# The high/low split of P^T and y^T writes their 32-token blocks as rows of 128

## The reference

```
# layer 0
Q = x @ Wq + bq ; K = ctx @ Wk + bk ; V = ctx @ Wv + bv
weights  = softmax(Q @ K^T * 512**-0.5, axis=keys)
x1 = x + (weights @ V) @ Wo + bo
# layer 1
q = x1 @ Wq + bq ; k = ctx @ Wk + bk ; v = ctx @ Wv + bv
w    = softmax(q @ k^T / sqrt(512), axis=tokens of x1)
x2   = x1 + w @ v
out  = (x2 - mean) * rsqrt(var + 1e-6) * gamma + beta      # over features
```

## Time and profile before

| | |
|---|---|
| three runs | 1252.03, 1254.40, 1256.06 us; median 1254.4 us |
| the profiled execution | 1254.56 us; its span 1252.8 us |
| TensorE busy (matmuls) | 1212.8 us, 97% of the span, 8304 matmuls |
| GpSimd, VectorE, ScalarE busy | 927.1, 892.0, 700.2 us |
| granted TensorE clock, mean | 0.987 |
| DMA | 241.36 MB, mean 193 GB/s |

### The profile page before, as it was taken

The page is one execution under the profiler, slowest core; times in us unless marked ns, Lnnn a source line. Parts: engine busy times, 40 slices in busy tenths (PEclk is TensorE's granted clock), DMA queues, the critical chain, the costliest instruction groups (busy, mean ns, idle before and its releaser), DMA issues.

```text
span 1252.8 us, 25385 instructions
## 1 busy us (share of the span) xinstructions
PE 1212.8 (97%) x8304; PEld 1122.5 (90%) x8304; DVE 892.0 (71%) x1874; ACT 700.2 (56%) x1545; POOL 927.1 (74%) x713
## 2 busy tenths in 40 slices
PE   6989999999999999999999999999999999999984
PEld 5779999999999999999999999999999999999973
DVE  1457777777777777777777777777777777767763
ACT  2436565655656565565656566555656655565542
POOL 2436778778877877787787778778777877877664
PEclk8999999999999999999999999999999999999988
DMA  8346666656655665665666566556655655665431
GB/s 327 108 137 211 187 197 214 206 173 216 219 185 197 212 210 172 213 220 178 204 210 212 170 212 222 186 195 212 216 169 206 224 193 186 215 199 176 151 118 50
DMA packets 121727, 241.36 MB, mean 193 GB/s; under 512 B 13920, under 2 KB 79456, under 8 KB 113120
## 3 DMA queue, kind: packets, MB, share of 16 engines
q1 hardware_dynamic: 120816, 240.18, 57.6%
q10 hardware_dynamic: 880, 0.79, 0.2%
HBM read 157.03 MB, written 83.89 MB: 192 GB/s over the span
## 4 chain that ended last, share of the span: by engine, by line
PE 89%; DMA 3%; DVE 3%; POOL 2%; issue 2%; ACT 1%; SPq 1%; ACTq 0%; POOLq 0%; DVEq 0%
PE bank L268 82%; PE bank L385 2%; PE bank L358 2%; DMA beta_b<-in_beta 1%; PE bank L337 1%; DMA yT_raw<-y_dram 1%; DVE stats L795 1%; DMA y_dram<-y_blk 1%; SPq L214 1%; PE bank L395 1%; PE bank L401 1%; DVE R L787 0%; POOL Y L956 0%; POOL yT_lo L908 0%; DVE y_blk L725 0%
## 5 line engine op out<-in xcount | busy, mean ns | idle before, releaser
L908 POOL TENSOR_TENSOR PT_lo<-PT_raw,PT_hi 128x512 fp32r<-128x512 f32 x64 | 82.7, 1292 | 192.4 <-ACT PT_hi L475 192.4
L596 ACT ACTIVATE Y<-R,nmr,rstd 128x512 f32<-128x512 f32 x128 | 97.4, 809 | 184.1 <-POOL nmr L948 184.1
L908 POOL TENSOR_TENSOR xT_lo<-IN,xT_hi 128x1024 fp32r<-128x1024 f32 x64 | 154.2, 2409 | 24.3 <-ACT xT_hi L475 24.3
L908 POOL TENSOR_TENSOR yT_lo<-yT_raw,yT_hi 128x1024 fp32r<-128x1024 f32 x64 | 154.4, 2412 | 23.2 <-ACT yT_hi L475 23.2
L956 POOL TENSOR_TENSOR Y<-Y,gamma_b 128x512 f32<-128x512 f32 x128 | 162.4, 1289 | 3.7 <-ACT Y L596 3.7
L959 POOL TENSOR_TENSOR Y<-Y,beta_b 128x512 f32<-128x512 f32 x128 | 163.1, 1297 | 0.0
L268 PE MATMUL bank<-yT_hi,A_hi 128*128 128x256 f32 x512 | 146.6, 286 | 5.4 <-POOL yT_lo L908 5.4
L268 PE MATMUL bank<-yT_hi,A_lo 128*128 128x256 f32 x512 | 147.4, 288 | 0.0
L268 PE MATMUL bank<-yT_lo,A_hi 128*128 128x256 f32 x512 | 146.7, 286 | 0.0
L268 PE MATMUL bank<-xT_hi,A_hi 128*128 128x256 f32 x512 | 144.1, 281 | 0.0
L268 PE MATMUL bank<-xT_lo,A_hi 128*128 128x256 f32 x512 | 144.0, 281 | 0.0
(11 more groups left out here) (116 smaller groups left out, 4204.8 us busy)
## 6 DMA issues: line engine op xcount, KB each, us to landing
IN<-in_packed SPq DMA_DIRECT2D x64, 1024.0 KB, 5.7
R<-in_x SPq DMA_DIRECT2D x64, 512.0 KB, 6.3
y_dram<-y_blk SPq DMA_DIRECT2D x256, 128.0 KB, 2.4
yT_raw<-y_dram SPq DMA_DIRECT2D x64, 512.0 KB, 3.6
out<-Y SPq DMA_DIRECT2D x64, 512.0 KB, 3.4
E_dram<-E_blk SPq DMA_DIRECT2D x256, 64.0 KB, 1.8
PT_raw<-E_dram SPq DMA_DIRECT2D x64, 256.0 KB, 2.6
WqT_s<-in_WqT SPq DMA_DIRECT2D x2, 1024.0 KB, 11.3
```

Source lines behind the costliest of these rows:

```text
L596: nc.scalar.activation(Y[n.k % 2][:, q, :], R[n.k % 4][:, q, :], ACT.Identity, bias=nmr[:, q:q + 1], scale=rstd[:, q:q + 1]).then_inc(Y_se ...
L908: return nc.gpsimd.tensor_tensor(dst, src, fp(hi), ALU.subtract)
```

## The change

The tensors `PT_hi`, `PT_lo`, `yT_hi` and `yT_lo` get the shape depth-and-half (q, k) x 128 tokens. The copy and the subtraction read `PT_raw` and `yT_raw` in the order (q k), i, t, which is 32-element runs (16 for P^T, 32 for y^T) at a stride, and write rows of 128 contiguous tokens; the subtraction reads the high part in that same contiguous order. `by_q` gives TensorE 2 runs of 128 contiguous elements in place of 2 x 4 runs of 32. Numbers of instructions, sizes of tensors, DMAs, waits and order stay.

```
-        PT = split("PT", [P, NB * ST, LT, 32])
+        PT = split("PT", [P, ST * LT, P])
-        yT = split("yT", [P, NB * ST, DT, 32])
+        yT = split("yT", [P, ST * DT, P])
...
         def by_q(t, k):
-            return t[:, :, k, :].rearrange("p (i q) t -> p q i t", q=ST)
+            return t[:, :, :].rearrange("p (q k) t -> p q k t", q=ST)[:, :, k, :]
+
+        def raw(t):
+            return t[:, :, :, :].rearrange("p (i q) k t -> p i (q k) t", q=ST).rearrange("p i c t -> p c i t")
+
+        def blocks(t):
+            return t[:, :, :].rearrange("p c (i t) -> p c i t", i=NB)
...
-                copy(flat4(PT[0]), flat4(PT_raw)).then_inc(PT_hi, 1)
+                copy(blocks(PT[0]), raw(PT_raw)).then_inc(PT_hi, 1)
...
-                copy(flat4(yT[0]), flat4(yT_raw)).then_inc(yT_hi, 1)
+                copy(blocks(yT[0]), raw(yT_raw)).then_inc(yT_hi, 1)
...
-                minus(flat4(PT[1]), flat4(PT_raw), flat4(PT[0])).then_inc(PT_lo, 1)
+                minus(blocks(PT[1]), raw(PT_raw), blocks(PT[0])).then_inc(PT_lo, 1)
...
-                minus(flat4(yT[1]), flat4(yT_raw), flat4(yT[0])).then_inc(yT_lo, 1)
+                minus(blocks(yT[1]), raw(yT_raw), blocks(yT[0])).then_inc(yT_lo, 1)
```

## The result

The changed kernel took 1248.2 us (median of 8 runs, 1246.89 to 1250.8) against 1254.3 us before (8 runs, 1252.03 to 1256.84): ratio 0.9949, 95% interval 0.9938 to 0.9959. It is 6.1 us faster (the interval says 5.1 to 7.8); forecast were 6.2. The profiled execution took 1247.58 us, its span 1245.8 against 1252.8.

A forecast was written before the change was run, and what follows sets the result against it. TensorE's matmul starts were taken as the bound, GpSimd's loop next. `v_` and `Pc_` together -0.10 us per body over 61 bodies, given as -6.2 us, other engines' costs covered: 1254.4 to 1248.2 us, range 1244.5 to 1256.5.

The forecast's parts named there:

- What bounds the kernel: Steady part: distances between TensorE matmul starts set the time, 18.24 us per body; GpSimd's loop second at 17.75 us.
- `v_`: 24 matmuls moving y^T: longer runs bring them near the pace of `u_`, saving 0.094 us per body.
- `Pc_`: 12 matmuls moving P^T: longer runs save 0.01 us per body, from one slow 0.13 us distance in each half.
- 6/7: Share of the 0.11 us gain counted for `v_`, as 1 of 7 joins between runs stays.
- ScalarE and GpSimd at nothing: Strided reads in copies and subtractions: 0.03 us growth on each engine, all covered by slack.
- Rival 2: GpSimd subtractions pay per run, slower: 29 us at 20 ns per run, some 475 us at 172 ns; chance 0.12.
- the loop that it would have hit: GpSimd, norm, `PT_hi`, `PT_lo` waiting on each other: 17.75 us per body, 0.49 us of slack.
- the pause before `rstd`: GpSimd's slack in its loop, 0.49 us per body; expected to shrink to about 0.36 us.
- Rival 1: Layout never set the matmul pace of `v_`: no change or small gains, 1254 us expected; chance 0.33.
- Rival 3: TensorE's new moving rows meet worse addresses, slower: +19 us, 1273 us; chance 0.03.

The follow-up runs named there:

- e1: Changed kernel with only y^T in rows of 128, P^T copied and read as before: 1251.36 us, ratio 0.9972 to the kernel before.
- e2: Changed kernel with only P^T in rows of 128, y^T as before: 1252.3 us, ratio 0.9989 to the kernel before.
- e4: Changed kernel with VectorE's transposes reordering blocks so products read one run of 256: 1248.85 us, ratio 0.9958 to the kernel before.
- e5: Changed kernel with `v_` and `Pc_` reading 4 runs of 64, elements in wrong order: 1247.94 us, one run.
- e8: Changed kernel with stationary matrices A0 and A1 exchanged between `u_` and `v_` from the fifth sequence on: 1247.69 us, one run.
- e9: Changed kernel with the loop's tensors except output buffers moved 32 bytes on; A0, A1, `Bv`, `V1` stay: 1240.35 us, one run.
- e10: Changed kernel with one additional 64-column instruction on GpSimd per body, result unread: 1249.59 us, one run.
- e11: Changed kernel with one additional 512-column instruction on GpSimd per body, result unread: 1287.42 us, one run.
- e3: Changed kernel's splits, but products read in the old pattern, 8 runs of 32, wrong order: 1254.67 us, ratio 1.0003 to the kernel before.

## Why the prediction was right

**What bounds the kernel: right.** TensorE's starts set the body; each nanosecond taken from `v_` and `Pc_` came out of it, in e1 and e2 separately.

**`v_`: right in kind, but a third of the term did not come.** The term was -94 ns, it measured -64. The step that was off is the row taken: I took the pace of `u_` as what contiguous rows give `v_`, and a join as the unit of cost. e4 and e5 show no cost of joins between runs of 64 or more, and that even one row of 256 leaves `v_` at 2851. So the 6/7 was wrong too; it only happened to bring the term nearer. The remaining 38 ns to `u_` are not a matter of runs, nor of which matrix is stationary (e8). They aren't fixed either: in e9 the order turns round, `v_` 2741, `u_` 2829. What they come from stays open. By the sizes declared x^T and y^T lie a multiple of 2 KiB apart, so the low part of the address doesn't tell them apart; what differs is the product ahead (`wc_` and `out_`), the bank written and the rest of the address. The nearest row was of the right shape, and nothing in the trace of before said that this isn't enough.

**`Pc_`: -10 forecast, -16 measured.** The clue taken, one matmul on `PT_lo` followed after 0.13 us twice per product, was a good one: in the changed kernel these two distances are 120 ns, before they were 129 (medians). The term was worked out as 0.01 for each of the two and then taken as 0.01 for both, which is where the missing 6 ns were.

**Not forecast: the neighbours.** `S1_` and `wc_` won 10 ns each, `s_` lost 7. That -13 together made good part of the 30 missing in `v_`. The body shrank by 93 ns where the forecast had 104 (-94 and -10), because misses of both signs met. That, and a forecast and a median 0.1 us apart when the interval is 5.1 to 7.8 us, is luck. A slip in the sum is small beside it: 61 x 0.10 is 6.1, not 6.2.

**ScalarE and GpSimd at nothing: right,** 0 to -5 ns where I allowed 30. Rival 2 with its 8.3 us was a bound far from the truth; the loop that it would have hit is real (e10, e11). The loop itself was mis-sized: it has three pauses, not two, and the pause before `rstd` went from 0.49 to 0.46 us, not to 0.36, as the one ahead of `C_lo` shrank as well, from 0.22 to 0.15.

**Rival 1** (the layout not the cause) fell with e3. **Rival 3** (addresses that meet badly) did not happen, but e9 shows that the place of the tensors counts, with the other sign.

**Open.** Why 32 bytes matter, and of which tensor, is not shown; no other shift was tried, so which places are best isn't known either. Nor is the reason for the step between runs of 64 and 32 in `v_` shown, or whether it is the length of the runs or the distance between them.

## What to carry to other kernels

Where TensorE is dense, read its pace from start to start, product by product, and compare products of the same form: in this kernel's steady part a few nanoseconds per matmul were all that was left to win. Try runs of 64 fp32 elements (256 bytes) or more in moving operands, since here no product that reads them was slower with long runs than with short ones, and let the engine that copies them anyway do the sorting, as its strided reads were free here; then try where the tensors lie, since a shift by 32 bytes was worth about 1 us with short runs and 7 us with long ones. Before loading more work on a second engine, find out which of its pauses belong to a loop of waits: only the others are slack, and all of those count, the short ones too.

## What the runs showed of the hardware that I had not expected

- A moving operand of 256 fp32r columns read in runs of 256, 128 or 64 elements gave identical distances; in runs of 32 or 16 the 24 matmuls of `v_` took 64 and 62 ns longer, and in runs of 32 the 24 of `u_` 117 ns. The 12 of `Pc_` took 16 ns longer with 32, 3 ns with 16. All this is from bodies at a granted clock of 1.00.
- Moving the tensors of the loop 32 bytes on changed the mean pace of `v_` from 118.8 to 114.2 ns per matmul (113 from the fourth on) and that of `u_` from 117.2 to 117.9 (e9).
- A product's pace can carry over: `S1_` (e2) and `wc_` (e1) changed by 10 ns with `Pc_` and `v_` ahead of them, their own operands untouched.
- VectorE's block transpose took an output order with four dimensions at the same speed: 1246 and 704 ns in e4, 1246 and 703 before.
